# The opening of a linear attention stage: raw weight loads behind the first gathered rows, output-side folds behind the low-rank product, memsets behind the gathers

## The reference

```
x = x + 0.5 * ffn0(layernorm(x))      # 64 experts, top 6, capacity 96, and a shared one
x = x + attn0(layernorm(x))           # gated linear attention, 8 heads
x = x + 0.5 * ffn0(layernorm(x))
x = x + 0.5 * ffn1(layernorm(x))      # 8 dense experts, top 2
x = x + attn1(layernorm(x))           # latent attention, 16 heads
x = x + 0.5 * ffn1(layernorm(x))
```

```
q = x @ Wq * DK**-0.5;  k = x @ Wk;  v = x @ Wv;  g = x @ Wg
gk = log_sigmoid(x @ Wgk0 @ Wgk1 + bgk1) / 16
S_t = S_{t-1} * exp(gk_t) + k_t v_t^T;  o_t = q_t S_t
o = o * rsqrt(mean(o*o) + eps) * g_norm_w * silu(g);  return o @ Wo
```

## Time and profile before

| | us |
|---|---|
| median of 3 runs (lowest to highest) | 1670.85 (1670.62 to 1672.13) |
| the profiled execution, its own time | 1665.35 |
| its span, first to last instruction | 1663.6 |
| first raw load issued to first fold | 279.92 to 298.92 |
| tile 0's rows added from | 294.35 |
| low-rank product, start and end on TensorE | 322.48 to 324.43 |
| tile 4's rows added from | 325.94 |

### The profile page before, as it was taken

The page is one execution under the profiler, slowest core; times in us unless marked ns, Lnnn a source line. Parts: engine busy times, 40 slices in busy tenths (PEclk is TensorE's granted clock), DMA queues, the critical chain, the costliest instruction groups (busy, mean ns, idle before and its releaser), DMA issues. The chain is left out here.

```text
span 1663.6 us, 39494 instructions
## 1 busy us (share of the span) xinstructions
PE 1424.6 (86%) x14334; PEld 984.3 (59%) x14334; DVE 1074.0 (65%) x2743; ACT 756.4 (45%) x1786; POOL 775.7 (47%) x741
## 2 busy tenths in 40 slices
PE   6879996647898996888999377878999999997898
PEld 3556664424555554455666256645667777676687
DVE  6862222577775654783222488958898888874888
ACT  5434443345556533553444212127776666662322
POOL 4554333754410000454333566508998888982000
PEclk9999998679899997989999689989999999999899
DMA  9309995421100002513998232200000000000000
GB/s 270 100 10 267 310 323 175 148 73 48 51 17 1 1 1 70 160 34 106 295 319 266 77 87 80 76 1 14 4 17 3 16 4 3 16 4 3 13 19 20
DMA packets 92664, 145.50 MB, mean 87 GB/s; under 512 B 25032, under 2 KB 52528, under 8 KB 92512
## 3 DMA queue, kind: packets, MB, share of 16 engines
q1 hardware_dynamic: 62816, 93.06, 18.9%
q0 software_dynamic: 15360, 37.77, 7.6%
q10 hardware_dynamic: 14336, 12.59, 2.7%
HBM read 122.39 MB, written 18.87 MB: 85 GB/s over the span
## 5 line engine op out<-in xcount | busy, mean ns | idle before, releaser
L2299 POOL TENSOR_TENSOR sb_m_prob<-sb_m_prob,sb_m_rinv 128x512 f32<-128x512 f32 x256 | 260.4, 1043 | 44.1 <-DVE sb_m_rinv L2349 40.4
L1273 POOL DMA_INDIRECT sb_c_rows<-slot_rows,sb_slot x192 | 193.4, 1007 | 97.9 <-issue 52.1
L2229 ACT ACTIVATE sb_m_prob<-m_ps_s,sb_m_nmax 128x512 f32<-128x512 f32 x256 | 173.8, 683 | 125.1 <-DVE sb_m_nmax L2355 124.4
L1106 POOL DMA_INDIRECT e_xn<-xn_rows,sb_table x128 | 118.0, 922 | 180.1 <-PE e_ps_x L1185 167.6
L1256 DVE TENSOR_TENSOR sb_e_h<-sb_e_sg,e_ps_gu 96x176 f32<-96x176 f32 x128 | 42.6, 333 | 226.9 <-ACT sb_e_sg L1232 226.9
L2355 DVE TENSOR_REDUCE sb_m_nmax<-m_ps_s 128x1 f32<-128x512 f32 x256 | 163.9, 682 | 29.4 <-PE m_ps_s L2133 26.9
L1194 PE MATMUL e_ps_gu<-e_wgu,sb_e_xT 128*96 128x352 f32 x512 | 172.8, 459 | 0.5 <-ACT sb_e_xT L1226 0.5
L2363 DVE STREAM_TRANSPOSE sb_m_pT<-sb_m_prob 128x1024 f32<-128x1024 f32 x128 | 157.6, 1232 | 0.0
L2146 PE MATMUL m_ps_v<-sb_m_pT,sb_m_lat_rows 32*64 32x128 f32 x8192 | 135.2, 273 | 5.6 <-issue 4.8
L2132 PE MATMUL m_ps_s<-sb_m_latT_high,sb_m_qa 128*128 128x512 f32 x256 | 125.6, 490 | 15.4 <-ACT sb_m_prob L2229 15.3
L2146 PEld LDWEIGHTS m_ps_v<-sb_m_pT,sb_m_lat_rows 32*64 32x64 f32 x8192 | 119.0, 130 | 29.1 <-issue 28.1
(11 more groups left out here) (280 smaller groups left out, 3072.4 us busy)
## 6 DMA issues: line engine op xcount, KB each, us to landing
e_wgu<-wgu SPq DMA_DIRECT2D x128, 352.0 KB, 6.7
e_wdn<-wdn SPq DMA_DIRECT2D x128, 192.0 KB, 6.8
slot_rows<-sb_e_y ACTq DMA_DIRECT2D x128, 96.0 KB, 6.1
xn_rows<-e_xn SPq DMA_DIRECT2D x16, 256.0 KB, 2.2
sb_c_rows<-slot_rows,sb_slot POOLq DMA_INDIRECT x192, 2.8
sb_x<-x SPq DMA_DIRECT2D x4, 512.0 KB, 5.3
e_xn<-xn_rows,sb_table POOLq DMA_INDIRECT x128, 6.4
sb_g_zm<-wqT SPq DMA_DIRECT2D x1, 2048.0 KB, 9.0
```

The source lines that it names most:

```text
L1106: pool.indirect_dma_start(x, None, k.xn_rows[:, :], bass.IndirectOffsetOnAxis(ap=k.table[:, e:e + 1], axis=0))\
L1273: pool.indirect_dma_start(rows[u][j][:, :], None, k.slot_rows[:, :], bass.IndirectOffsetOnAxis(ap=k.slot[:, n, j:j + 1], axis=0))\
L2229: act.activation(prob[s % 4][:, hh, :], ps_s[j % 3][:, :], ACT.Exp, bias=nmax[s % 2][:, hh:hh + 1], accum_out=rsum[s % 2][:, hh:hh + 1]).t ...
L2299: pool.tensor_tensor(part, part, rinv[s % 2][:, hh:hh + 1].to_broadcast([P, T]), ALU.mult)\
```

## The change

Four edits in one function. The sync engine waits, before its three loads, until the six gathers of tile 0 have landed. TensorE no longer waits for `same_head` at its start but at its first use, `mean_squares(0)`, in slot 1. The output folds and their copies come after the low-rank product and its copy. GpSimd makes `same_head` after the gathers of the first eight tiles.

```diff
@@ -1373,6 +1373,7 @@
         @block.sync
         def _(sp):
+            sp.wait_ge(k.sem("c_rows_got0"), 16 * TOPK)
             for dst, name in ((wqT, "wqT1"), (upT, "upT1"), (wo1, "wo1")):
                 sp.dma_start(dst, k.w[name].rearrange("(h p) d -> p h d", p=DH)).then_inc(raw_loaded, 16)
@@ -1527,6 +1528,8 @@
             def mean_squares(u):
+                if u == 0:
+                    pe.wait_ge(made, 1 + HG)
                 pe.wait_ge(sq_ready, u + 1)
@@ -1611,13 +1614,14 @@
             pe.wait_ge(k.sem("w0_loaded"), W0)
-            pe.wait_ge(made, 1 + HG)
             pe.wait_ge(w_high, 2)
             pe.wait_ge(raw_loaded, 48)
-            for n in range(FOLDS):
+            for n in range(ABSORBS):
                 fold(n)
             transposes(0)
             low_rank(0)
+            for n in range(ABSORBS, FOLDS):
+                fold(n)
             pe.wait_ge(w_low, 1)
@@ -1765,11 +1769,13 @@
-            for n in range(FOLDS):
+            for n in range(ABSORBS):
                 fold_copy(n)
             deviations(0)
             xT_copies(0)
             low_copy(0)
+            for n in range(ABSORBS, FOLDS):
+                fold_copy(n)
@@ -1788,13 +1794,13 @@
             pool.sem_inc(k.sem("c_rows_used"), 2)
+            for n in range(2 * TB):
+                gather(n)
             pool.memset(same_head[:, :], 0.0).then_inc(made, 1)
             pool.wait_ge(made, 1)
             for i in range(HG):
                 pool.memset(same_head[i * DV:(i + 1) * DV, i * DV:(i + 1) * DV], 1.0).then_inc(made, 1)
             pool.wait_ge(made, 1 + HG)
-            for n in range(2 * TB):
-                gather(n)
```

## The result

The changed kernel has a median of 1675.91 us (1670.8 to 1687.95, 16 runs), the kernel before, measured beside it, 1671.77 (1665.56 to 1678.25, 16 runs). The ratio is 1.0033, 95% interval 1.0017 to 1.0050: slower, by about 4.1 us of median, or 5.5 by the ratio; 6.5 (0.39%) was predicted and lies within the interval. The forecast of 1677.3 stood on a median of 1670.85. The interval also holds the +4.5 (0.27%) of rival B, the full clock; the times alone do not choose between A and B, the trace does.

A forecast was written before the change was run, and what follows sets the result against it. Bound by two chains meeting within 0.2 us at ScalarE's deviations, tile 3's rows and folds, then by tile 4 to tile 6 and VectorE. 9.7 + 0.7 - 5.9 + 2.0 = +6.5 us on 1670.85: 1677.3, range 1673.8 to 1679.8.

The forecast's parts named there:

- rival B: Transposes and low-rank product find the full 2.4 GHz clock, so +4.5 us, 1675.3; chance 0.17.
- A: The forecast itself: lateness at the deviations plus the clock term, +6.5 us, 1677.3; chance 0.60.
- output folds and copies not ahead of deviations: TensorE and ScalarE in the opening: output folds and copies no longer stand ahead of the deviations, -5.9 us.
- The trigger: First gather at 280.4, tile 0 landed at 289.6 with 2.8 for landing, so raw loads start +9.7 us later.
- The length of the loads: Raw loads to first fold take +0.7 us, with two or three more gathers in the transfer; bounds -1.5 and +1.5.
- Where it meets the other chain: At ScalarE's deviations: the fourth fold copy, ending at 323.84, sets their start, +4.5 us; tile 3's rows come earlier.
- Rival E: Faster: the rows of the opening decide and come 2.7 us earlier, giving 1668.2; chance 0.04.
- The clock: TensorE's transposes and low-rank product run at 1.2 GHz behind the absorb folds, +2.0 us, bounds 0 and +2.7.
- Output folds behind the product: Ahead of the gates they take 5.8 us, last copy up to 0.3; the 6.25 slack covers it, cost nothing.
- Rival C: The gates decide: the last logarithm passes the 6.25 us slack, adding 1 to 2 us, 1679; chance 0.08.
- Memsets: On GpSimd between the gathers of tiles 7 and 8, some 1.8 us, covered by 7 us: cost nothing.
- To the end of the kernel: Low_parts' lateness passes through tile 4, tile 6's gathers and VectorE's unbroken run to the stage's end, +6.5 us.

The follow-up runs named there:

- x3_memsets_only: Kernel before with only the memsets moved behind the gathers, TensorE waiting for them at mean_squares(0); 1670.39 us against 1671.75, ratio 1.0017.
- x6_after_tile4: Changed kernel with tile 4's rows added ahead of low_parts(0); 1674.34 us against 1669.82 for the kernel before, ratio 1.0013.
- x1_wait_only: Kernel before with only the sync engine's wait for tile 0's rows ahead of the three raw loads; 1682.79 us against 1671.75, ratio 1.0068.
- x2_no_wait: Changed kernel without the sync engine's wait, memsets and output folds still moved; 1674.24 us against 1671.75 for the kernel before, ratio 1.0025.
- x7_wo_late: Changed kernel with only wo1's load waiting for tile 0, wqT and upT loaded at once; 1674.33 us against 1669.82 for the kernel before, ratio 1.0015.
- x5_tile4_first: Kernel before with memsets behind the gathers and tile 4's rows added between normalise(0) and low_parts(0); 1668.08 us against 1669.82, ratio 0.9981.
- x4_filler: Changed kernel with four extra 512-column matmuls on TensorE ahead of the absorb folds; 1672.73 us against 1671.75 for the kernel before, ratio 1.0015.
- x8_combined: Changed kernel without wait, two output folds ahead of transposes, tile 4 ahead of low_parts, gate_sums ahead of tile 6's rows; 1665.53 us against 1668.18 before, ratio 0.9979.

## Why the prediction was right

The time and its sign were right, and the terms came out one by one, measured at the same places, so the sum is not right by errors that cancel:

```
term                                             predicted   measured
first raw load later                                +9.7       +9.98
loads take longer, issue to first fold              +0.7       +0.53
output folds and copies not ahead of deviations     -5.9       -6.03
                          deviations later          +4.5       +4.48
transposes and product at 1.2 GHz                   +2.0       +2.12
                          low_parts later           +6.5       +6.60
                          slot -2 later                        +6.71
                          last output later                    +6.76
```

**The trigger.** I took 280.4 for the first gather, as if half of the 0.89 ahead of it before were not the memsets' doing. It starts at 280.83, 0.80 after the stage, and in x3_memsets_only 0.81 after it: of the 1.79 us between the stage's start and the first gather before the change, removing the memsets frees 1.0. The landing of 2.8 taken from the earlier trace rows was right (2.75).

**The length of the loads.** 19.53 for 19.00. The term has the right sign and size, but its reason (two or three more gathers within the transfer) is not shown: x6_after_tile4, whose opening is the same up to there, took 19.15, and x1_wait_only 19.27, x2_no_wait 18.48, x3_memsets_only 19.05. The scatter is as large as the term.

**Where it meets the other chain.** Shown from both sides. With the wait alone (x1_wait_only) the deviations are late by 10.7 and start behind the last fold copy; without it (x2_no_wait) or with the folds early (x7_wo_late) ScalarE waits for the rows, by 3.86 and 11.81. Rival E's premise, rows 2.7 earlier, holds where nothing is held back (2.6 in x2_no_wait, 2.4 in x3_memsets_only). In the changed kernel it is 1.65, since tile 1 now waits behind the loads, and even that ends in VectorE's idle 6.73.

**The clock.** From the deviations to low_parts it is 5.7 to 5.85 us in the four kernels that have all eight folds ahead (before, x1_wait_only, x3_memsets_only, x5_tile4_first) and 7.8 to 8.1 in the six others: +2.0 to +2.4 wherever some or all output folds stand behind, with the wait or without. Rival B, the full clock, is out. The Trainium skill, "TensorE: Matmul & The Clock Gate", part 1, would release the clock by sustained activity; 13.55 us of busy time in 14.00 at 0.50 do not agree, so for these instructions the measurement decides. That the loss goes with the order of the folds is shown in all ten traces; why was not settled. It is not the idle time ahead of the transposes alone: that is 1.89 us before and 1.57 in x1_wait_only, with the product at the full clock, and 1.56 after and in x4_filler, with the product at half. In x2_no_wait (5.53) and x7_wo_late (13.52) a longer idle time stands there, and these two cannot tell the idle time from the folds. x8_combined leaves that open even more: with two output folds ahead the clock was at 1.00 over the transposes and at 0.50 over the product.

**Output folds behind the product.** I priced them at 5.8 us and at a last copy of 0.3, in a slack of 6.25. They took 3.65, from 331.00 to the gates at 334.65, with the clock up as they run (0.91 in 330.00:334.00). The logarithm ends at 343.74 and the scan starts at 347.81, so 4.07 of slack remain. They cost nothing, as said, but with more room than said; x6_after_tile4 shows the other side of that slack as a wait of 3.63. Rival C did not occur.

**Memsets.** Nothing, as said: x3_memsets_only.

**To the end of the kernel.** The shift passes to the stage's end in the changed kernel (+6.71 at slot -2, +6.76 at the last output) and nearly so in x1_wait_only (+10.80 and +10.35). This is less strict than I had put it. x7_wo_late is 0.56 late at slot -2 and 2.1 early at the last output. The later slots have stretches at 1.2 GHz that differ from one trace to another: the low-rank product that starts 172 us into the stage took 3.78 us before and in x2_no_wait and 3.06 in x7_wo_late, and the last group of output matmuls 6.68 to 6.74 in the kernels before, after, x1_wait_only, x2_no_wait and x8_combined, and 5.11 in x7_wo_late. So two us at the stage's end are no evidence on the opening, and the timed ratios of the experiments, whose intervals all hold 1 but for that of x1_wait_only, tell less than their milestones, each of which is from one trace. That the profiled span grew by 12.4 where the stage grew by 6.8 lies outside the stage and was not traced to a cause.

## What to carry to other kernels

Before holding a load back for the sake of a faster one, find the instruction where the two chains meet: here they met within 0.2 us, so delaying one by 10 cost 10, less what was taken off the path beside it, and freeing the other gave nothing. A hold should apply only to the transfer that is not needed early: with wo1 alone held, the folds were off the path, and the opening lost 0.6 us instead of 6.7. When independent matmuls are moved from ahead of a critical product to behind it, read in a trace at which clock the product then runs, for what it loses there comes off what the move gives (2.1 of 6.2 us here); and look for an idle engine's next piece of work that frees a buffer (tile 4's rows in x5_tile4_first, 3 us within the stage, though its timed interval holds 1) before touching the transfers.

## What the hardware showed beside that

- The absorb folds (16 products of 64 columns each) follow one another every 3.4 us at a granted clock of 0.50, and every 1.8 at 1.00 (x4_filler). In x7_wo_late TensorE was busy with them for 13.88 us of 13.90, at 0.50 throughout.
- The granted clock fell while TensorE was at work: in x4_filler from 0.99 to 0.50 between 321.52:322.52 and 322.52:323.52, in the middle of the transposes, behind folds at 1.00 (7.24 busy in 8.70) and 1.56 of idle; it stayed at 0.50 over a product that kept TensorE busy 3.97 of 4.00.
- It also changed between two stretches with an idle time of 1.62 between them: 0.50 over two output folds that kept TensorE busy all of 3.70 us, 1.00 over the transposes next (x8_combined).
- A gather's landing depends on what runs beside it: from the issue of tile 0's last one to the use of its rows it was 2.75 us with no raw load under way, 5.9 with them.
- An indirect gather that is the first instruction of GpSimd in the stage starts 0.80 us after the stage does; where memsets of 0.9 us in all stand ahead of it, 1.79.
